# Sending expert results back to their tokens by indirect store, slot by slot, in the second of two fused transformer layers

## The chip, the core and the metric

The kernel is one program on one core of a Trainium2 chip. The metric is the device time of one execution in microseconds (us). Five engines run side by side, each through its own list of instructions in order: PE (TensorE), DVE (VectorE), ACT (ScalarE), POOL (GpSimd) and SP (SyncE, which here only issues DMAs). They wait for each other through semaphores. An engine that waits holds up everything behind it in its own list.

## The reference, cut to what matters

Two layers over 8 sequences of 512 tokens of 128 floats. Each layer is attention over the normalised tokens, then a mixture of 8 experts, each with a residual sum:

```
x = x + attention_0(layernorm(x))     # 16 heads of 8, causal
x = x + experts_0(layernorm(x))       # top 1 of 8 experts, gated SiLU, hidden 512
x = x + attention_1(layernorm(x))     # latent keys and values, rotary, causal
x = x + experts_1(layernorm(x))       # top 2 of 8 experts, ReLU, hidden 512, biases
```

In layer 1 a token's output is the sum over its two experts of probability times `relu(x @ w1[e] + b1[e]) @ w2[e] + b2[e]`. All of it is float32.

## The kernel before, in words

**Batches and halves.** X holds all 4096 tokens on chip, as 32 tiles of 128 tokens by 128 floats, for the whole kernel. Attention goes one sequence (a "batch", 4 tiles) at a time, 16 times in all (8 batches by 2 layers). The experts go by halves: once the attention of four batches (16 tiles) is done, the routing of their 2048 tokens is worked out and their experts run, beside the attention of the following batches. The last half of layer 1 has no attention beside it; it is the end of the kernel.

**One half of the experts.** (1) `route`, `choose` and `places` (PE, ACT, mostly DVE) pick the experts of each token and give each pair of token and choice k a row in a list sorted by expert, padded for each expert to a multiple of 128 rows. The row numbers are `rows_of[g][k]`, one column for each tile. The list has 23 blocks of 128 rows ("slots") in layer 0 and 39 in layer 1, the most that the padding can need. (2) `scatter` (L1090): POOL writes each tile of normalised tokens to its rows of `sorted_in` in DRAM by an indirect DMA of 64 KB, 16 of them in a half of layer 0 and 32 in a half of layer 1 (two for each tile). (3) `fetch` (L1004): SP loads four slots at a time; the first waits for all scatters of the half (L1000). `turn_rows` (L1277) transposes them on PE. (4) For each slot `fetch_w1` (L993) loads the weights of its expert, `first` (L1294) and `second` (L1304) are its two matmul stages on PE, ACT takes the ReLU (L1452), and DVE adds the bias `b2` and writes the result to `rows_out` (L1689, whose records carry L1467). `rows_out` is a ring of three buffers of two slots each. (5) SP stores two slots at a time to `sorted_out` in DRAM (L1014). (6) `combine` (L1100): once all the stores of the half have landed, POOL gathers for each tile and each k the 128 result rows by an indirect DMA into one of four `gathered` buffers, 32 gathers in a half of layer 1, and DVE adds each, times its gate, to X (L1698). A gather waits until the one four before it has been added (L1099). (7) `store` (L1020): SP writes a batch of X to the output, 256 KB.

Before layer 0's first scatter the lists in DRAM are filled with zeros, 39 slots for each half, by ten DMAs from one zero tile (`FILLS`, L964 to L970), as both layers share the lists.

**What sets the order.** Each engine's list is written down before anything runs. `schedule` gives every step a due time from constants (`FIRST_SCORES`, `LENGTHS`, `HURRY`, `SCATTER`, `EXPERTS_AFTER`, `SLOT`, `COMBINE`). `Plan.make_orders` then plays the steps through with costs in us (`PARTS`, `LANDS`) and the dependences of `needs`: again and again it takes the step that can start soonest, and among those that can start equally soon the one with the earliest due time. An indirect DMA counts 1.0 us of POOL there. The costs only choose the order; on the chip the engines follow that order as their semaphores allow.

Due times in layer 1 before the change, worked out from the constants: half 1's 32 scatters at 734 to 766, 1.0 apart; half 0's slots at 685 to 807, 3.12 apart.

Of the kernel before, what the change touches and what calls it, by code (L numbers as in the profile page):

```python
# [58 lines left out]
C_ALL = 332  # L59
# [26 lines left out]
W1_AHEAD = 8.06  # L86
DMA = 16
@dataclass
# [32 lines left out]
class Timetable:  # L121
# [84 lines left out]
    def scatter(self, layer, g, x, at, each):  # L206
        for t in range(QT * x, QT * x + QT):
            for k in range(TOPK[layer]):
                self.put(at, "scatter", layer, g, x, (t, k))
                at += each  # L210
        return at

    def combine(self, layer, g, x, at, each):
        for t in range(QT * x, QT * x + QT):
            for k in range(TOPK[layer]):
                self.put(at, "combine", layer, g, x, (t, k))
                at += each
        if layer == 1:
            self.put(at, "store", layer, g, x)
        return at  # L220
# [16 lines left out]
def schedule():  # L237
# [6 lines left out]
    for n, at in enumerate(FILLS):  # L244
        table.put(at, "fill", x=n)
    starts, end = [], 0.0
    for n, length in enumerate(LENGTHS):
# [20 lines left out]
        if b % GB == GB - 1:  # L268
            g = b // GB
            for x in range(GB):  # L270
                chosen = table.scatter(layer, g, x, chosen, SCATTER[layer][g])
# [23 lines left out]
    "second": (("pe", 0.9), ("dve", 0.24), ("sp", 0.5)), "combine": (("pool", 1.0), ("dve", 0.35)), "store": (("sp", 0.5),)}  # L295

PARTS_L1 = {"first": (("pe", 0.9), ("act", 1.2)), "choose": (("dve", 6.8),), "places": (("pe", 0.2), ("dve", 6.4))}
# [4 lines left out]
         "fetch_w1": 4.6, "fetch": 3.0, "second": 2.4, "combine": 2.5}  # L302
# [12 lines left out]
class Plan:  # L315
# [18 lines left out]
    def parts(self, s):  # L334
# [9 lines left out]
        if s.kind == "second" and s.x % OUT_GROUP != OUT_GROUP - 1 and s.x != SLOTS[s.layer] - 1:  # L344
            return parts[:2]
# [30 lines left out]
    def needs(self, s, engine):  # L376
# [113 lines left out]
        if s.kind == "scatter":  # L490
            return done("dve", of("places", layer, b)) + done("act", of("norm", layer, GB * b + x, "half")) + done("sp", of("fill", x=len(FILLS) - 1)) + (
                done("sp", of("fetch", 0, b, (SLOTS[0] - 1) // 4)) if layer else [])
# [24 lines left out]
        if s.kind == "second":  # L517
            if engine == "pe":
                return done("act" if layer else "dve", of("first", layer, b, x))
            if engine == "dve":  # L520
                out = []
                if x % OUT_GROUP == 0 and s.turn:
                    old = [k for k in self.by_kind["second"] if k.x % OUT_GROUP == 0 and (k.slot, k.turn) == (s.slot, s.turn - 1)][0]
                    out = done("sp", of("second", old.layer, old.b, min(old.x + OUT_GROUP - 1, SLOTS[old.layer] - 1)))
                return out
            return done("dve", self.last_combine(0, b)) if layer and x < OUT_GROUP else []
# [5 lines left out]
        if s.kind == "store":  # L532
            return done("dve", of("combine", 1, b, x, (QT * x + QT - 1, TOPK[1] - 1)))
# [18 lines left out]
    def make_orders(self):  # L552
# [32 lines left out]
        while left:  # L585
# [17 lines left out]
            s.done[engine] = at + us + (LANDS.get(s.kind, 0.0) if engine == "sp" or (engine == "pool" and s.kind in ("scatter", "combine")) else 0.0)  # L603
# [67 lines left out]
def two_layers(nc, d):  # L671
    with ExitStack() as ctx:
# [41 lines left out]
        rows_in = [sb(f"rows_in{i}", [P, SEQ])[:, :] for i in range(2)]  # L714
# [5 lines left out]
        xn_half = sb("xn_half", [P, GT, DIM])  # L720
# [23 lines left out]
        slot_f = sb("slot_f", [1, MAXSLOTS])  # L744
        gates = [[sb(f"gate{g}{k}", [P, GT]) for k in range(2)] for g in range(HALVES)]
        rows_of = [[sb(f"rows_of{g}{k}", [P, GT], I32) for k in range(2)] for g in range(HALVES)]
# [1010 lines left out]
```

## Time and profile before

| | |
|---|---|
| median of 3 runs | 1118.13 us (1117.6 to 1125.34) |
| the profiled execution | 1108.93 us, its span 1107.1 us |
| PE busy | 934.3 us (84%) |
| DVE busy | 691.2 us (62%) |
| ACT busy | 617.4 us (56%) |
| POOL busy | 466.9 us (42%) |
| share of the chain that ended last: PE, DVE, POOL, DMA | 56%, 13%, 10%, 6% |

The span runs from the first instruction to the last event of the execution. A busy share is an average over it; the chain is the work followed back from the last instruction, at each step to what released it. An indirect DMA has two times: POOL's own, while it makes the descriptors, and the time to landing, counted from the issue until the data is there.

### The profile page before, as it was taken

The page shows a single profiled execution, that of the slowest core. Times are in us where ns is not written, and L with a number is a line of the kernel's source. Part 1 is how long each engine was busy: PE and PEld are TensorE (multiplying, and loading weights), DVE is VectorE, ACT ScalarE, POOL GpSimd, SP SyncE. Part 2 cuts the span into 40 slices and gives each one's busy share as a digit, 9 for nine tenths or more (in the row PEclk, how much of TensorE's full clock was granted, in tenths as well). Part 3 has the DMA queues.
Part 4 walks back from the last instruction along what each step waited for, and adds up shares of the span by engine and source line. Part 5 has one row for each costly group of instructions (what it writes and reads, how often), then busy time and mean ns, then how long its engine had stood idle before and what let it go on. Part 6 is the DMA issues. An engine that isn't in the chain of part 4 may idle for free.

```text
span 1107.1 us, 26573 instructions
## 1 busy us (share of the span) xinstructions
PE 934.3 (84%) x9732; PEld 623.3 (56%) x9732; DVE 691.2 (62%) x1454; ACT 617.4 (56%) x1148; POOL 466.9 (42%) x632
## 2 busy tenths in 40 slices
PE   4879989987999998987999888988989997579920
PEld 2434445444887644544877544453447687578920
DVE  4866887787545897987546888888775124023122
ACT  4147786762544576863444576784667864245610
POOL 3033334245111585456111586346862213773046
PEclk9759999996999998998999989997899998889975
DMA  4626433236665124445643214425332456678822
GB/s 134 143 80 185 129 78 80 57 96 187 188 175 153 41 63 117 93 152 166 204 152 106 57 56 117 117 62 144 103 83 70 120 153 171 195 199 235 242 61 74
DMA packets 148045, 139.42 MB, mean 126 GB/s; under 512 B 35056, under 2 KB 126544, under 8 KB 147920
## 3 DMA queue, kind: packets, MB, share of 16 engines
q1 hardware_dynamic: 141776, 125.13, 41.5%
q0 software_dynamic: 6144, 12.60, 4.0%
q8 instruction: 82, 1.34, 0.5%
q14 instruction: 43, 0.35, 0.1%
HBM read 94.82 MB, written 42.86 MB: 124 GB/s over the span
## 4 chain that ended last, share of the span: by engine, by line
PE 56%; DVE 13%; POOL 10%; issue 8%; DMA 6%; ACT 6%; SPq 1%; POOLq 0%; ACTq 0%; DVEq 0%
PE psum L1294 13%; PE psum L1227 11%; PE psum L1304 10%; DVE neg_max L1470 8%; PE psum L1209 5%; PE psum L1185 4%; ACT scratch L1416 4%; POOL sorted_in L1090 4%; DMA gathered<-sorted_out,rows_of 3%; POOL gathered L1100 3%; PE psum L1237 2%; POOL scratch L1077 2%; PE psum L1120 1%; PE psum L1262 1%; PE psum L1188 1%
## 5 line engine op out<-in xcount | busy, mean ns | idle before, releaser
L1470 DVE TENSOR_REDUCE neg_max<-psum 128x2 f32<-128x768 f32 (+3 forms) x352 | 382.5, 1120 | 77.7 <-PE psum L1190 76.1
L1416 ACT ACTIVATE scratch<-psum 128x1024 f32<-128x1024 f32 x320 | 318.3, 1026 | 100.0 <-PE psum L1209 99.3
L1077 POOL TENSOR_SCALAR_AFFINE_SELECT scratch<-scratch 128x512 f32<-128x512 f32 x256 | 159.6, 640 | 357.1 <-ACT scratch L1416 356.7
L1185 PE MATMUL psum<-k_stack,q_stack 48*128 48x128 bf16 (+3 forms) x1024 | 156.3, 328 | 34.7 <-DVE neg_max L1470 23.6
L1227 PE MATMUL psum<-scratch,values 128*32 128x512 f32 (+3 forms) x2048 | 173.7, 464 | 12.1 <-POOL scratch L1077 9.9
L1294 PE MATMUL psum<-rows_t,w_now 128*128 128x128 f32 x1360 | 179.2, 283 | 1.6 <-issue 1.0
L1294 PEld LDWEIGHTS psum<-rows_t,w_now 128*128 128x128 f32 x1360 | 165.1, 196 | 12.0 <-issue 10.3
L1209 PE MATMUL psum<-q_stack,k_stack 51*128 51x512 bf16 (+3 forms) x1024 | 126.6, 315 | 24.8 <-ACT scratch L1416 9.5
L1304 PE MATMUL psum<-w,hidden_t 128*128 x992 | 138.1, 283 | 10.7 <-DVE rows_out L1467 9.2
L1304 PEld LDWEIGHTS psum<-w,hidden_t 128*128 128x128 f32 x992 | 121.8, 193 | 23.0 <-issue 22.5
L1452 ACT ACTIVATE hidden_t<-psum,w_now 128x128 f32<-128x128 f32 x312 | 88.6, 369 | 69.2 <-PE psum L1294 62.5
L1100 POOL DMA_INDIRECT gathered<-sorted_out,rows_of x96 | 92.4, 963 | 82.1 <-DMA sorted_out<-rows_out 51.5
L1090 POOL DMA_INDIRECT sorted_in<-xn_half,rows_of x96 | 93.0, 969 | 51.9 <-issue 26.3
L1188 PE MATMUL psum<-masks_bf 64*128 64x128 bf16 x1024 | 114.5, 235 | 0.0
L1185 PEld LDWEIGHTS psum<-k_stack,q_stack 48*128 48x128 bf16 x1024 | 53.4, 98 | 99.8 <-DVE neg_max L1470 39.0
L1227 PEld LDWEIGHTS psum<-scratch,values 128*32 128x32 f32 x2048 | 57.7, 114 | 80.5 <-issue 47.7
L1190 PE MATMUL psum<-masks_bf 64*128 64x64 bf16 x1024 | 101.4, 200 | 0.0
L1698 DVE SCALAR_TENSOR_TENSOR X<-gathered,gate,X 128x128 f32<-128x128 f32 x96 | 36.2, 377 | 78.4 <-DMA gathered<-sorted_out,rows_of 77.7
L1467 DVE TENSOR_TENSOR rows_out<-psum,w_now 128x128 f32<-128x128 f32 x78 | 22.6, 291 | 97.7 <-PE psum L1304 97.7
L1209 PEld LDWEIGHTS psum<-q_stack,k_stack 51*128 51x128 bf16 x1024 | 36.3, 96 | 80.7 <-issue 35.2
L1312 ACT ACTIVATE ctx_raw<-psum 128x512 f32<-128x512 f32 x64 | 38.1, 595 | 75.1 <-PE psum L1227 75.0
L1190 PEld LDWEIGHTS psum<-masks_bf 64*128 64x128 bf16 x1024 | 56.7, 105 | 32.2 <-issue 9.8
(118 smaller groups left out, 1051.2 us busy)
## 6 DMA issues: line engine op xcount, KB each, us to landing
w_now<-in_w SPq DMA_DIRECT2D x78, 322.0 KB, 3.6
w_now<-in_w SPq DMA_DIRECT2D x46, 512.0 KB, 4.3
q_stack<-q_parts SPq DMA_DIRECT2D x64, 192.0 KB, 4.1
sorted_out<-rows_out SPq DMA_DIRECT2D x60, 128.0 KB, 3.0
rows_in<-sorted_in SPq DMA_DIRECT2D x28, 256.0 KB, 3.3
q_parts<-q_parts SPq DMA_DIRECT2D x16, 384.0 KB, 2.9
k_stack<-k_parts SPq DMA_DIRECT2D x32, 192.0 KB, 3.7
q_parts<-q_parts SPq DMA_DIRECT2D x16, 256.0 KB, 3.1
```

What stands on the lines that cost most here:

```text
L1077: pool.affine_select(out=diag, in_=diag, compare_op=ALU.is_ge, fill=0.0, base=0, pattern=[[0, 4], [1, P]], channel_multiplier=-1).then_inc ...
L1090: pool.indirect_dma_start(sorted_in[g][:, :], bass.IndirectOffsetOnAxis(ap=rows_of[g][k][:, t:t + 1], axis=0), xn_half[:, t, :], None).the ...
L1100: pool.indirect_dma_start(gathered[s.slot][:, :], None, sorted_out[g][0:SLOTS[s.layer] * P, :], bass.IndirectOffsetOnAxis(ap=rows_of[g][k] ...
L1185: pe.matmul(out[:, j * width:end], q_stack[i][rows, pair, t * P:(t + 1) * P], k_stack[i][rows, k_of(layer, pair), 0:width], start=True, st ...
L1188: pe.matmul(out[:, end - P:end], ident_up[half, :], mask_up[half, :], start=False, stop=False)
L1190: ins = pe.matmul(out[:, end - P // 2:end], ident_low[half, :], mask_low[half, :], start=False, stop=True)
L1209: ins = pe.matmul(bank[u.bank + k][:, off:off + SEQ - j * P], k_stack[i][rows, k_of(layer, pair), j * P:(j + 1) * P], q_stack[i][rows, pai ...
L1227: ins = pe.matmul(bank[u.bank][CW * c:CW * c + CW, j * P:SEQ], values[batch_of(s) % 3][:, j, col:col + CW], p[:, c % 2, off:off + SEQ - j ...
L1294: ins = pe.matmul(bank[v.bank][:, c * P:(c + 1) * P], w1_now[layer][w.slot][:, n * FFN + c * P:n * FFN + (c + 1) * P], rows)
L1304: ins = pe.matmul(bank[u.bank][:, 0:P], hidden_t[h.slot][:, k * P:(k + 1) * P], w2[layer][:, bass.ds(e, 1), k * DIM:(k + 1) * DIM].rearran ...
L1416: act.activation(expd[s.slot], psum[:, u.bank:u.bank + 2, :], ACT.Exp, scale=SCALE).then_inc(read[u.bank], 1)
L1470: return dve.tensor_reduce(out=out, in_=in_, axis=AX, op=op, negate=negate)
```

## The change

Layer 1's results no longer go through `sorted_out` and gathers. Rows of `sorted_in` in layer 1 get a 129th float (`ROW`), the place that the result must go to: `C_TOKEN` holds the number of each token in its half, DVE copies it into the new column of `xn_half` in `places`, and after the scatters of k = 0 of a batch a new DVE step, `mark`, adds 2048 to it for k = 1 (after waiting until those scatters have landed). The order of scatters becomes: all 16 of k = 0, then all 16 of k = 1. After each `fetch` DVE waits for the load and copies the 129th column to `goes_to` as integers. For each slot of layer 1 POOL then issues one indirect store of 64 KB from `rows_out` to `returned` in DRAM, at the places of `goes_to`; rows of padding go to a part of `returned` that nothing reads. The 40 stores of layer 1 on SP are gone. `take_back` replaces the 64 gathers of layer 1: for each batch SP issues two plain loads of 256 KB (k = 0 and 1) into the `scratch` that attention uses, after all sends of the half have landed and the last attention is over (`values_made`); DVE waits for both and makes 8 multiply-adds. The lists in DRAM are separate for each layer now: layer 0's have 23 slots (six fills of zeros), layer 1's are filled from a new input `empty_rows` by ten DMAs from DRAM to DRAM, due at 300 to 390. Layer 0 keeps its stores and gathers. Several constants of the due times are other ones.

```diff
-FILLS = (75.0, 80.0, 85.0, 90.0, 95.0, 100.0, 105.0, 115.0, 125.0, 135.0)
+FILLS = ((75.0, 80.0, 85.0, 90.0, 95.0, 100.0), (300.0, 310.0, 320.0, 330.0, 340.0, 350.0, 360.0, 370.0, 380.0, 390.0))
-FIRST_SCORES = 77.59
-AHEAD = (74.87, 87.27)
+FIRST_SCORES = 80.02
+AHEAD = (92.93, 87.27)
-LENGTHS = (41.61, 37.6, 36.08, 35.9, 45.3, 45.3, 45.3, 41.6, 44.0, 44.0, 44.0, 44.0, 34.43, 38.0, 38.0, 38.0)
+LENGTHS = (41.61, 37.6, 37.45, 35.9, 45.3, 45.3, 45.3, 41.35, 44.0, 44.0, 44.0, 44.0, 34.43, 38.0, 38.0, 37.51)
-HURRY = ((30.0, 30.0), (5.73, 36.79))
-SCATTER = ((1.8, 1.1), (1.73, 1.0))
-EXPERTS_AFTER = ((6.0, 5.52), (12.95, 6.0))
-SLOT = ((2.56, 2.6), (3.12, 1.47))
-COMBINE = ((2.44, 2.0), (2.0, 0.2))
+HURRY = ((30.0, 30.0), (2.52, 12.84))
+SCATTER = ((1.8, 1.1), (1.73, 2.32))
+EXPERTS_AFTER = ((6.0, 5.52), (12.95, 21.95))
+SLOT = ((2.47, 2.6), (2.87, 1.47))
+COMBINE = ((3.03, 2.0), (1.31, 0.67))
-W1_AHEAD = 8.06
+W1_AHEAD = 6.52
+ROW = DIM + 1
+RETURNED = 2 * GT * P
...
+    def scatter(self, layer, g, at, each):
+        for k in range(TOPK[layer]):
+            for x in range(GB):
+                if k:
+                    self.put(at - each, "mark", layer, g, x)
+                for t in range(QT * x, QT * x + QT):
+                    self.put(at, "scatter", layer, g, x, (t, k))
+                    at += each
+        return at
...
+        if layer == 1:
+            self.put(at, "take_back", layer, g, x)
+            at += QT * TOPK[layer] * each
+            self.put(at, "store", layer, g, x)
+            return at
...
+    "mark": (("dve", 0.2),), "take_back": (("sp", 1.0), ("dve", 3.3))}
+PARTS_L1 = {"fetch": (("sp", 0.5), ("dve", 0.2)), "second": (("pe", 0.9), ("dve", 0.24), ("pool", 1.0)), ...
...
+        if s.kind == "take_back" and engine == "sp":
+            return done("pool", of("second", 1, b, SLOTS[1] - 1)) + done("pe", of("values", 1, BATCHES - 1, 3, 1))
... SP:
+                    else:
+                        sp.dma_start(out, d["empty_rows"][first * P:(first + n) * P, :]).then_inc(filled[1], DMA)
...
+                elif s.kind == "take_back":
+                    g, x = s.b, s.x
+                    if x == 0:
+                        for slot, value in enumerate(sends_made(g)):
+                            sp.wait_ge(sent_back[slot], value)
+                        sp.wait_ge(values_made, 4 * 2 * BATCHES)
+                    for k in range(2):
+                        first = (k * GT + QT * x) * P
+                        sp.dma_start(taken_back(g, x, k), returned[g][first:first + QT * P, :].rearrange("(t p) d -> p t d", p=P)
+                                     ).then_inc(back_loaded[g][x], DMA)
... POOL:
+                        pool.wait_ge(filled[s.layer], FILLED[s.layer])
+                    if t == QT * x and k == 1:
+                        pool.wait_ge(marked, of("mark", 1, g, x).n + 1)
...
+                elif s.kind == "second":
+                    g, u = s.b, s.uses[0]
+                    x = s.x % OUT_GROUP
+                    slot = of("second", 1, g, s.x - x).slot
+                    pool.wait_ge(places_known, places_read(of("turn_rows", 1, g, s.x // 4)))
+                    pool.wait_ge(read[u.bank], u.after)
+                    pool.indirect_dma_start(returned[g][:, :], bass.IndirectOffsetOnAxis(ap=goes_to[g][:, s.x:s.x + 1], axis=0),
+                                            rows_out[slot][:, x * P:(x + 1) * P], None).then_inc(sent_back[slot], DMA)
... DVE:
+                elif s.kind == "fetch":
+                    n = rows_of_group(1, s.x)
+                    dve.wait_ge(fetched[s.slot], DMA * (s.turn + 1))
+                    dve.tensor_copy(goes_to[b][:, 4 * s.x:4 * s.x + n],
+                                    rows_in[s.slot][:, 0:n * ROW].rearrange("p (t n) -> p t n", t=n)[:, :, DIM]).then_inc(places_known, 1)
+                elif s.kind == "mark":
+                    x = s.x
+                    dve.wait_ge(scattered[x], marks_sent(b, x))
+                    to = xn_half[:, QT * x:QT * x + QT, DIM]
+                    dve.tensor_scalar(to, to, float(GT * P), None, ALU.add, ALU.bypass).then_inc(marked, 1)
+                elif s.kind == "take_back":
+                    g, x = b, s.x
+                    dve.wait_ge(back_loaded[g][x], 2 * DMA)
+                    for k in range(2):
+                        for t in range(QT):
+                            row = X[:, g * GT + QT * x + t, :]
+                            ins = dve.scalar_tensor_tensor(out=row, in0=taken_back(g, x, k)[:, t, :], scalar=gates[g][k][:, QT * x + t:QT * x + t + 1],
+                                                           in1=row, op0=ALU.mult, op1=ALU.add)
+                        if k == 0:
+                            settle(ins)
+                    ins.then_inc(added, 1)
```

## Rows read from the trace of the kernel before

**Rows 1.** The page's forty slices of 27.7 us: busy tenths of PE.

```profile
PE   4879989987999998987999888988989997579920
```

**Rows 2.** Windows by stage: start and end, length, busy us (instructions) by engine, clock, DMA share, GB/s.

```profile
902.00:928.00 26.00, 21.05 (x176) 19.66 (x175) 14.03 (x55) 14.86 (x49) 1.47 (x3) 0.99 0.57 161
...
957.00:972.00 15.00, 0.00 (x0) 0.00 (x0) 0.59 (x2) 0.00 (x0) 11.38 (x12) 0.65 0.49 151
...
1010.00:1060.00 50.00, 49.14 (x419) 47.65 (x419) 8.50 (x30) 30.39 (x103) 0.94 (x1) 1.00 0.77 211
1060.00:1107.00 47.00, 0.00 (x0) 0.00 (x0) 11.43 (x33) 0.00 (x0) 30.35 (x32) 0.54 0.26 69
```

**Rows 3.** The same windows for the second matmul stage alone, line 1304 (8 instructions a slot).

```profile
902.00:928.50 26.50, 9.93 (x72) 8.74 (x72) 0.98 0.56 158
928.50:957.00 28.50, 15.63 (x104) 14.13 (x104) 0.90 0.77 216
...
979.00:1009.90 30.90, 13.96 (x104) 12.51 (x104) 1.00 0.82 229
```

**Rows 4.** Timeline of POOL: start, duration, operation [idle before]; half 1's scatters, first gathers.

```profile
927.74 1.04 POOL L1090 DMA_INDIRECT sorted_in<-xn_half,rows_of  x1 [21.39 <-DVE rows_of L1654]
...
966.98 0.96 POOL L1090 DMA_INDIRECT sorted_in<-xn_half,rows_of  x1 [0.30 <-issue]
968.24 0.99 POOL L1100 DMA_INDIRECT gathered<-sorted_out,rows_of  x1 [0.31 <-issue]
```

**Rows 5.** Timeline of PE around the start of half 1's experts.

```profile
972.23 2.27 PE L1277 MATMUL psum<-consts,rows_in 128*128 128x128 f32 x8 [15.32 <-DMA rows_in<-sorted_in]
...
979.07 1.06 PE L1304 MATMUL psum<-w,hidden_t 128*128 x8
```

**Rows 6.** The chain that ended last: start us, us, what; experts of half 1.

```profile
1005.22 3.90 DMA gathered<-sorted_out,rows_of
...
1009.41 0.29 DVE rows_out L1467
...
1009.95 1.15 PE psum L1304 x8
```

**Rows 7.** The same chain, from the last slot to the end.

```profile
1058.71 1.17 PE psum L1304 x8
...
1059.90 0.30 DVE rows_out L1467
...
1060.22 1.54 DMA sorted_out<-rows_out
...
1062.35 0.94 POOL gathered L1100
...
1103.77 0.35 DVE X L1698
```

**Rows 8.** DMA issues: number, KB each, median us to landing.

```profile
rows_in<-sorted_in SPq DMA_DIRECT2D x28, 256.0 KB, 3.3
...
sorted_in<-xn_half,rows_of POOLq DMA_INDIRECT x96, 2.2
```

**Rows 9.** Line 1077 (causal masks) alone, beside half 0's experts.

```profile
840.00:902.00 62.00, 11.72 (x19) 1.00 0.43 120
```

**Rows 10.** Timeline of POOL: half 0's scatters, the first and the sixteenth.

```profile
755.74 1.08 POOL L1090 DMA_INDIRECT sorted_in<-xn_half,rows_of  x1 [1.26 <-DVE rows_of L1654]
...
787.31 0.96 POOL L1090 DMA_INDIRECT sorted_in<-xn_half,rows_of  x1 [0.30 <-issue]
```

**Rows 11.** The costliest groups of the page: DVE's row maxima, and its adds of gathered rows.

```profile
L1470 DVE TENSOR_REDUCE neg_max<-psum 128x2 f32<-128x768 f32 (+3 forms) x352 | 382.5, 1120 | 77.7 <-PE psum L1190 76.1
...
L1698 DVE SCALAR_TENSOR_TENSOR X<-gathered,gate,X 128x128 f32<-128x128 f32 x96 | 36.2, 377 | 78.4 <-DMA gathered<-sorted_out,rows_of 77.7
```

More of the change, by code:

```diff
@@ L204, in after @@
         return at + 23.0 + 4.0 * layer
[L206 to L210, printed above, removed]
+    def scatter(self, layer, g, at, each):
[6 more added lines that the diff above has]
+                    at += each
         return at
     def combine(self, layer, g, x, at, each):
-        for t in range(QT * x, QT * x + QT):
[L215 to L219, printed above, removed]
+        if layer == 1:
[3 more added lines that the diff above has]
+            return at
+        for t in range(QT * x, QT * x + QT):
+            self.put(at, "combine", layer, g, x, (t, 0))
+            at += each
         return at
@@ L243, in schedule @@
         table.put(REST_AT + 0.4 * n, "load_rest", x=n)
-    for n, at in enumerate(FILLS):
-        table.put(at, "fill", x=n)
+    for layer, times in enumerate(FILLS):
+        for n, at in enumerate(times):
+            table.put(at, "fill", layer, x=n)
     starts, end = [], 0.0
@@ L269, in schedule @@
             g = b // GB
-            for x in range(GB):
-                chosen = table.scatter(layer, g, x, chosen, SCATTER[layer][g])
+            chosen = table.scatter(layer, g, chosen, SCATTER[layer][g])
             end = table.experts(layer, g, max(chosen + EXPERTS_AFTER[layer][g], end + 12.0), SLOT[layer][g])
@@ L490, in needs @@
         if s.kind == "scatter":
-            return done("dve", of("places", layer, b)) + done("act", of("norm", layer, GB * b + x, "half")) + done("sp", of("fill", x=len(FILLS) - 1)) + (
-                done("sp", of("fetch", 0, b, (SLOTS[0] - 1) // 4)) if layer else [])
+            return done("dve", of("places", layer, b)) + done("act", of("norm", layer, GB * b + x, "half")) + done("sp", of("fill", layer, x=len(FILLS[layer]) - 1)) + (
+                done("dve", of("mark", 1, b, x)) if y[1] else [])
+        if s.kind == "mark":
+            return done("pool", of("scatter", 1, b, x, (QT * x + QT - 1, 0)))
         if s.kind == "fetch_w1":
@@ L792, in two_layers @@
         W2_LOADED = EXPERTS * DMA
-        ZERO_FILLED = len(FILLS) * DMA
+        FILLED = [len(times) * DMA for times in FILLS]
         def batch_of(s):
@@ L1024, in _ @@
                 sp.wait_ge(out_stored, DMA * BATCHES)
-            for slot, value in enumerate(stores_made(1, 1)):
+            for slot, value in enumerate(stores_made(HALVES - 1)):
                 sp.wait_ge(stored[slot], value)
@@ L1683, in _ @@
                     dve.wait_ge(full[u.bank], u.filled)
[L1684 to L1685 removed]
+                    if x == 0 and stores_before(head, 0):
+                        dve.wait_ge(stored[head.slot], stores_before(head, 0))
+                    if x == 0 and stores_before(head, 1):
+                        dve.wait_ge(sent_back[head.slot], stores_before(head, 1))
                     if layer == 0:
```

135 lines of the change are left out of this document (80 added, 55 removed).

## The prediction

> **What bounds the kernel now.** I read the page's slices first: PE is 8 or 9 tenths busy nearly everywhere until the last six slices, where it falls to 5 and 7 and then to 2 and 0 [rows 1]. So up to about 900 us PE has work waiting, and an edit elsewhere is worth little there. The windows by stage divide the end. From 957 to 972 us PE does nothing (0.00 of 15.00), from 1010 to 1060 it is full (49.14 of 50.00), from 1060 to the end it is idle again for 47 us while POOL works 30.35 of them [rows 2]. Three things lie behind these windows. First, the scatters of half 1: POOL issues 32 from 927.74 to the last at 966.98 [rows 4], which is (966.98 - 927.74) / 31 = 1.266 us each, and PE's first transposes start at 972.23, after an idle time of 15.32 [rows 5]. Second, the gathers of half 0, behind those scatters on POOL [rows 4]: in the chain, DVE's write of a slot's result at 1009.41 stands behind a gather's landing of 3.90 us, and PE's next stage begins at 1009.95 [rows 6]. Third, the 32 gathers of half 1: the last slot's result is written at 1059.90, the first gather starts at 1062.35, the last add at 1103.77 [rows 7].
>
> **The sum** is made in the profiled execution, 1108.93 us with a span of 1107.1. The median of the three runs, 1118.13, is 9.2 above it; I take the difference over to that median.
>
> *The tail.* Now from the end of the last write, 1059.90 + 0.30, to 1107.1: 46.9 us [rows 7]. After the change: POOL's wake 0.3 and a store whose nearest row is the scatter, also 64 KB and indirect, 2.2 us to landing [rows 8], makes 2.5. SP's wake 0.2. Then eight loads of 256 KB in the form of the row fetches, 3.3 us alone [rows 8]. Beside each other they are bound by bandwidth: the experts' windows move 211 GB/s [rows 2], 262 KB at that rate is 1.25 us. So the pair of batch 0 is there after 3.3 + 1.25 = 4.6 and the last pair after 3.3 + 7 x 1.25 = 12.1. DVE has 8 adds a batch; one takes 0.377 on the mean and 0.35 here [rows 7, 11], 2.8 a batch, 11.2 for four. DVE ends at 4.6 + 11.2 = 15.8 (by the loads it would be 12.1 + 2.8 = 14.9). The last output takes 1107.1 - 1104.1 = 3.0 [rows 7]. Sum 2.5 + 0.2 + 15.8 + 3.0 = 21.5; gain **25.4**. From below: adds that overlap at 0.27, then bandwidth binds, 20.6. From above: loads at half the rate, 2.5 each, end at 20.8, then 2.8 and 3.0: 29.3.
>
> *Half 1's experts.* With half 0's gathers gone the slots run at their own pace. From 1009.95 to 1058.71 it is 25 slots in 48.76 us, 1.95 each [rows 6, 7]. From 979 to 1009.9 it was 104 / 8 = 13 slots in 30.9 us [rows 3], 25.4 at that pace: gain **5.5**. The start-up (972.23 to 979.07 [rows 5], at a lower clock: 0.65 is granted in the idle window before it [rows 2]) stays. POOL's send is 1.27 a slot, under 1.95, and falls beside PE's work. Half 0's take_back needs its last send, 32 adds (11.2 us of DVE) and 2 MB of loads; they find PE idle in front of half 1's start, so I cost them at nothing. If half 0's sends end so late that this cover is gone, they lie in half 1's run, where DVE is busy 8.50 of 50 [rows 2], and cost at most their 11.2.
>
> *The scatters of half 1, the part that speaks against the change.* POOL was free for them. Now it also sends half 0's slots, and the fetch waits for the last scatter. Line 1304 has 9 slots from 902 to 928.5 and 13 from 928.5 to 957 [rows 3]; the last of the nine gets its result out only behind `places`, so 14 sends fall in the time of the scatters. The order on POOL is by due time when both are ready: sends 26 to 38 are due at 772 to 807 (692 + 2.87 for each slot, and 5.5), scatters at 761 to 833 (2.32 apart). So all sends are written ahead of the last 12 scatters, and the scatters end 14 x 1.266 = **17.7** later. From below: scatters first, 0. From above: POOL waits at each send for PE's slot, 14 x 1.95 = 27.3. I take 17.7, since per slot one send and one and a half scatters are 3.2 us, more than PE's 1.95, so POOL is the late one and doesn't wait. PE's idle time becomes 15 + 17.7 = 33.
>
> *Earlier sends.* 17 of half 0's slots come before 902 and 8 before 928, 25 x 1.27 = 32 us of POOL. Beside attention POOL is a fifth busy (11.72 of 62 with masks [rows 9]). 17 sends make a third more; a mask that finds one in front of it waits 0.6 on the mean, so 19 masks lose about 4 us together, and PE has slots to do meanwhile. I count **1**; if each is paid in full with its landing order, 8; nothing in the trace makes it a gain beyond the SP time of 20 stores, which no one waits for.
>
> *Fills, columns, copies.* Ten fills of zeros become six, and ten of 528 KB are added in a stretch that PE fills; 0 to 3, I take 0. A longer row changes no count of DMAs. The copy of 39 x 128 places, the token column (0.1 to 0.2 on the way to the scatters) and the marks are 0.5 together if nothing waits; what waits is a rival. The Trainium skill has a rule against the longer rows: in "DMA: Bandwidth & Descriptors", "How a descriptor splits into AXI transactions", a descriptor that doesn't start on a 256-byte boundary starts its first read at the boundary below. A row of 516 bytes then costs about 24 beats where 512 took 16, an estimate from that section; by it the first fetch of half 1 would take 1.5 times as long, and the sum would be 1.7 us worse. No row shows an unaligned load, so the sum does without it.
>
> Sum: -25.4 - 5.5 + 17.7 + 1 + 0.5 = **-11.7**, which is 1106.4 on the median, 1106 rounded.
>
> **Rivals.**
> (B) *The scatters give more back.* POOL's order is worked out with 1.0 us for a send and 0.9 + 0.9 for a slot, the chip needs 1.27 and 1.95, and a DVE waiting in `mark` for a landing holds the results that the sends wait for. At the upper bound of the term, 27.3, and 3 for the early sends: -25.4 - 5.5 + 27.3 + 3 + 0.5 = -0.1; half way it is -6. Time 1112 to 1118, no change that counts. For: the due times put sends and scatters side by side. Against: POOL is the later of the two there.
> (C) *Slower: DVE waits for DMAs in half 0's scatters.* `mark` waits on DVE for POOL's scatters of k = 0, 16 of which take from 755.74 to 788 [rows 10], 32 us with other work between, where the written order allows 1.0 us each. Behind a waiting mark stand the row maxima, 1.12 us each [rows 11], and attention's PE behind them. Each us that DVE stands in this stretch counts in full, since the experts of half 0 haven't begun. It decides when the waits sum to more than 11.7 + 11.2 = 23 us. At 25 the time is 1131. Against: a mark is due 12 scatters before its own k = 1 scatter, so the planner may write it late.
> (D) *The term doesn't exist.* If the order puts scatters first, PE works through its 15 us of idle time and the sends trail: 0 in place of 17.7, -29.4, 1089.
>
> **How the numbers follow.** A measurement of this kernel can tell about 1%, 11.2 us, from no change. Forecast (A), 1106 with its own range from 1097 to 1111: 0.42. B: 0.36. C: 0.16. D: 0.06. A lies right at the edge of 1%, so part of its chance belongs to "within 1%" and nearly none of B's to faster: faster 0.42 + 0.06 less 0.04 = 0.44; within 1%: 0.36 + 0.04 + 0.02 (a mild C) = 0.42; slower 0.14. The range must hold A, B and the mild part of C: 1094 (the lower bounds of the tail and of the sends) to 1126; outside are D and the rest of C, 0.2.
>
> **What would show it.** The last `rows_out` is written 11 to 13 us later than 1060; from there to the end it is 21 us, not 47. Between the first and last scatter of half 1 POOL has 14 sends and 57 us instead of 40. PE's idle time ahead of half 1's experts is about 33 us. The pace from the first slot on is 1.95. The start of half 0's experts and the end of attention (902) stay within 3 us; if attention ends much later and DVE shows waits for `sorted_in`, it is C. If the scatters end at 968 as now, it is D. I am wrong above all if POOL waits in the middle of the scatters for PE, or if the loads of take_back are far slower beside each other than 1.25 us.

## The result, and the profile after

The changed kernel takes **1102.59 us** in the median of 18 runs (1096.22 to 1109.76); the kernel before, in 18 runs beside it, 1113.32 us (1101.77 to 1125.34). The ratio is 0.9919, 95% interval 0.989 to 0.9948: faster, by 0.5 to 1.1%. By the ratio that is 9.0 us less, where 11.7 were forecast, and 1106 was forecast from a first median of 1118.13, which the 18 runs put at 1113.32. The 11.7 taken from 1113.32 would have been 1101.6, so part of the nearness of 1106 to 1102.59 is that first median. The time lies in the range. The gain of 0.8% lies within the 1% that the prediction counted as no change, which it gave 0.42; it gave "faster" 0.44.

The profiled execution has a span of 1101.7 us against 1107.1. The windows by stage, cut at the changed kernel's own landmarks (columns as in [rows 2]: start and end, length, busy us and instructions of PE, PE's weight loads (PEld), DVE, ACT and POOL, then clock, DMA share, GB/s; "clock" is the granted TensorE clock as a share of full speed):

```profile
913.00:939.00 26.00, 21.41 (x180) 20.02 (x178) 14.11 (x57) 15.07 (x49) 9.95 (x11) 1.00 0.56 161
939.00:968.00 29.00, 25.96 (x195) 25.02 (x196) 5.26 (x21) 13.29 (x46) 22.01 (x23) 0.88 0.68 184
968.00:1002.00 34.00, 0.62 (x6) 0.43 (x4) 9.43 (x34) 0.00 (x0) 22.48 (x23) 0.53 0.56 166
1002.00:1083.00 81.00, 80.10 (x663) 77.69 (x663) 13.05 (x49) 49.45 (x166) 36.04 (x38) 0.96 0.71 199
1083.00:1101.70 18.70, 0.00 (x0) 0.00 (x0) 9.14 (x33) 0.00 (x0) 1.30 (x2) 0.59 0.60 176
```

Against [rows 2]: the first window does the same PE work as before, 21.41 us for 21.05, but begins at 913 instead of 902. PE's idle window is 34 us long instead of 15. Then half 1's experts fill PE for 80.10 of 81 us, and what follows the last slot is 18.7 us instead of 47.

The timeline of POOL shows why the idle window has grown (columns as in [rows 4], which these answer):

```profile
939.09 0.96 POOL L1147 DMA_INDIRECT sorted_in<-xn_half,rows_of  x1 [2.99 <-DVE rows_of L1753]
...
944.13 0.96 POOL L1156 DMA_INDIRECT returned<-rows_out,goes_to  x1 [0.30 <-issue]
945.40 0.95 POOL L1147 DMA_INDIRECT sorted_in<-xn_half,rows_of  x1 [0.30 <-issue]
946.66 0.96 POOL L1156 DMA_INDIRECT returned<-rows_out,goes_to  x1 [0.30 <-DVE goes_to L1556]
...
996.36 0.96 POOL L1147 DMA_INDIRECT sorted_in<-xn_half,rows_of  x1 [0.30 <-issue]
```

Scatters (L1147) and sends (L1156) are mixed until 981 us, and the last 12 scatters stand alone, as the due times said. There is the same 0.30 us between any two, so POOL never waits. From the first scatter to the last it is 57.3 us, where it was 39.2 [rows 4]: that is 14 sends of 1.266 us, 17.7, and 0.3 more. On PE's side (rows like [rows 5]):

```profile
967.47 1.15 PE L1371 MATMUL psum<-w,hidden_t 128*128 x8 [0.42 <-ACT hidden_t L1519]
1002.12 2.00 PE L1344 MATMUL psum<-consts,rows_in 128*128 128x128 f32 x8 [33.50 <-DMA rows_in<-sorted_in]
1003.92 4.77 PE L1361 MATMUL psum<-rows_t,w_now 128*128 128x128 f32 x24
1008.53 1.06 PE L1371 MATMUL psum<-w,hidden_t 128*128 x8
```

The idle time is 33.50, the forecast said "about 33". The chain that ended last, from the last slot to the end (columns as in [rows 6]; it answers to [rows 7]):

```profile
1080.41 0.91 PE psum L1371 x8
...
1083.96 2.23 DMA returned<-rows_out,goes_to
...
1086.21 0.38 SPq L1073
...
1087.74 4.41 DMA scratch<-returned
...
1092.17 1.15 DVE X L1572 x4
...
1093.35 2.20 DVE X L1572 x8
...
1095.57 2.20 DVE X L1572 x8
```

No POOL instruction stands between two adds any more. DVE goes through the four batches almost without a pause; the timeline of DVE there (same columns as POOL's) has one wait before the first batch and 0.18 before the rest:

```profile
1089.68 2.31 DVE L1572 SCALAR_TENSOR_TENSOR X<-scratch,gate,X 128x128 f32<-128x128 f32 x8 [6.47 <-DMA scratch<-returned]
...
1092.17 6.76 DVE L1572 SCALAR_TENSOR_TENSOR X<-scratch,gate,X 128x128 f32<-128x128 f32 x24 [0.18 <-DMA scratch<-returned]
```

The balance of the two profiled executions, in stages that add up to the span:

| stage | before | after | difference | forecast |
|---|---|---|---|---|
| start to half 1's first scatter | 927.74 | 939.09 | +11.4 | +1.5 |
| first scatter to PE's first transposes of half 1 | 44.5 | 63.0 | +18.5 | +17.7 |
| to the end of the last `rows_out` | 88.0 | 81.1 | -6.9 | -5.5 |
| to the end of the span | 46.9 | 18.5 | -28.4 | -25.4 |
| sum | 1107.1 | 1101.7 | -5.4 | -11.7 |

Three of the four stages are as forecast within about 3 us. The first is not: attention's last projection ends 11 us later, and nothing in the forecast put it there (it begins at 913.0, before at 901.6). The experiments go after that, and after the largest loss, the 18.5.

### The profile page after: what moved, and what is told of

Read it like the earlier page. It is cut to its first block, busy times and chain, and to the rows that moved or that the text cites. A ratio compares the mean times of both kernels' runs of the same rounds, so it can differ in the third digit from the quotient of the medians.

```text
span 1101.7 us, 26611 instructions
## 1 busy us (share of the span) xinstructions
PE 942.7 (86%) x9732; PEld 626.8 (57%) x9732; DVE 695.3 (63%) x1484; ACT 617.3 (56%) x1148; POOL 480.5 (44%) x646
## 4 chain that ended last, share of the span: by engine, by line
PE 60%; DVE 11%; POOL 11%; ACT 7%; issue 7%; DMA 3%; SPq 1%; POOLq 0%; DVEq 0%; ACTq 0%
PE psum L1361 14%; PE psum L1293 12%; PE psum L1371 11%; DVE neg_max L1537 7%; POOL sorted_in L1147 6%; PE psum L1275 5%; PE psum L1251 4%; ACT scratch L1483 4%; PE psum L1222 2%; POOL scratch L1136 2%; PE psum L1303 2%; PE psum L1186 1%; PE psum L1254 1%; PE psum L1328 1%; PE psum L1344 1%
## 5 line engine op out<-in xcount | busy, mean ns | idle before, releaser
L1293 PE MATMUL psum<-scratch,values 128*32 128x512 f32 (+3 forms) x2048 | 183.2, 486 | 13.6 <-POOL scratch L1136 10.9
L1251 PE MATMUL psum<-k_stack,q_stack 48*128 48x128 bf16 (+3 forms) x1024 | 153.8, 324 | 35.7 <-DVE neg_max L1537 24.0
L1156 POOL DMA_INDIRECT returned<-rows_out,goes_to x78 | 75.1, 962 | 88.6 <-DVE rows_out L1534 66.4
L1293 PEld LDWEIGHTS psum<-scratch,values 128*32 128x32 f32 x2048 | 60.3, 117 | 86.7 <-issue 53.8
L1147 POOL DMA_INDIRECT sorted_in<-xn_half,rows_of x96 | 93.2, 971 | 32.3 <-issue 25.8
L1534 DVE TENSOR_TENSOR rows_out<-psum,w_now 128x128 f32<-128x128 f32 x78 | 22.9, 294 | 115.0 <-PE psum L1371 111.8
L1100 POOL TENSOR_TENSOR ln_small<-ln_small,consts 128x4 f32<-128x4 f32 x40 | 42.2, 1054 | 31.5 <-DVE ln_small L1604 31.2
```

Of the source, the lines that this page charges most:

```text
L1147: pool.indirect_dma_start(sorted_in[s.layer][g][:, :], bass.IndirectOffsetOnAxis(ap=rows_of[g][k][:, t:t + 1], axis=0), xn_half[:, t, 0:wi ...
L1251: pe.matmul(out[:, j * width:end], q_stack[i][rows, pair, t * P:(t + 1) * P], k_stack[i][rows, k_of(layer, pair), 0:width], start=True, st ...
L1293: ins = pe.matmul(bank[u.bank][CW * c:CW * c + CW, j * P:SEQ], values[batch_of(s) % 3][:, j, col:col + CW], p[:, c % 2, off:off + SEQ - j ...
```

## The experiments

The experiments ran in three groups. The kernels of a group shared one chip and their runs of the kernel before, and each has its own ratio to it. In the first group the kernel before took 1202.0 us, in the others 1112.64 and 1115.3. The first and the second group both carry the chip number 6, the third 9, so it isn't shown that the slow group ran on another chip than the second. Kernels of different groups are compared by their ratios, and the first group with care. Where a text below speaks of "that chip" or "the slower chip", read the first group.

### First group: where the constants, the fills and the order stand

**scatters_first**, sends written behind all scatters of half 1; only due times differ:

```diff
-SCATTER = ((1.8, 1.1), (1.73, 2.32))
-EXPERTS_AFTER = ((6.0, 5.52), (12.95, 21.95))
+SCATTER = ((1.8, 1.1), (1.73, 0.1))
+EXPERTS_AFTER = ((6.0, 5.52), (12.95, 92.99))
```

> The changed kernel with one thing altered: the 32 scatters of half 1 are due 0.1 apart instead of 2.32, so POOL has all of them ahead of half 0's remaining sends (the due time of half 1's experts is kept). Theory: sends and scatters share POOL, and each of the 14 sends written ahead of the last scatter puts off half 1's experts by 1.266 us. Then the scatters take 40.5 us again instead of 57.3, and PE's first transposes of half 1 come some 44.5 us after the first scatter instead of 63.0. The ring of six result slots makes PE leave about 8 slots of half 0 (15.6 us) for afterwards, which lie in what was idle time: the end comes 3 to 17 us earlier, 1 to 13 us if the sends left over then crowd half 1's first slots. Rival: PE's idle time is only moved behind half 0's late slots, since half 1's first slot can't pass them in PE's order: no difference, within 4 us of the changed kernel.

**old_times**, the changed kernel with all due-time constants of the kernel before:

```diff
-FIRST_SCORES = 80.02
-AHEAD = (92.93, 87.27)
+FIRST_SCORES = 77.59
+AHEAD = (74.87, 87.27)
...
-HURRY = ((30.0, 30.0), (2.52, 12.84))
-SCATTER = ((1.8, 1.1), (1.73, 2.32))
+HURRY = ((30.0, 30.0), (5.73, 36.79))
+SCATTER = ((1.8, 1.1), (1.73, 1.0))
...
```

> The changed kernel with every due-time constant of the kernel before (FIRST_SCORES, AHEAD, LENGTHS, HURRY, SCATTER, EXPERTS_AFTER, SLOT, COMBINE, W1_AHEAD). It also has the scatters of half 1 ahead of half 0's last sends. Theory 1: the 11 us by which attention of layer 1 ends later in the changed kernel's trace come from the new constants; then attention's last projection is back at 902 +- 3 us and the time is that of scatters_first less up to 11 us. Theory 2: they come from the change itself (fills from DRAM, DVE's waits for fetches, sends on POOL); then the last projection stays at 910 to 914. Theory 3: they are the scatter of single executions; then the projections of all these kernels vary by some us with no order.

**before_new_times**, the kernel before with the new constants for all that is ahead of layer 1's experts:

```diff
-FIRST_SCORES = 77.59
-AHEAD = (74.87, 87.27)
+FIRST_SCORES = 80.02
+AHEAD = (92.93, 87.27)
...
-SLOT = ((2.56, 2.6), (3.12, 1.47))
-COMBINE = ((2.44, 2.0), (2.0, 0.2))
-W1_AHEAD = 8.06
+SLOT = ((2.47, 2.6), (3.12, 1.47))
+COMBINE = ((3.03, 2.0), (2.0, 0.2))
+W1_AHEAD = 6.52
```

> The kernel before, with the changed kernel's constants for everything ahead of half 0 of layer 1's experts (FIRST_SCORES, AHEAD, LENGTHS, W1_AHEAD, layer 0's SLOT and COMBINE); stores, gathers, fills are as before. Theory 1 (new constants cost 11 us by the end of attention): last projection at 910 to 914, time 5 to 11 us over the kernel before. Theories 2 and 3: last projection at 898 to 905, time within 4 us of the kernel before.

**fills_early**, layer 1's fills moved on SP's queue:

```diff
-FILLS = ((75.0, ...), (300.0, 310.0, 320.0, 330.0, 340.0, 350.0, 360.0, 370.0, 380.0, 390.0))
+FILLS = ((75.0, ...), (120.0, 125.0, 130.0, 135.0, 140.0, 145.0, 150.0, 155.0, 160.0, 165.0))
```

> The changed kernel with layer 1's ten fills from DRAM due at 120 to 165 instead of 300 to 390; only SP's order differs. If the fills' traffic holds up the attention of batches 5 and 6 of layer 0 (where the changed kernel lost 8 us of its lead), the projections of those batches come up to 8 us earlier and the time is 3 to 8 us less. If the fills cost nothing, as the prediction took them, it is within 3 us of the changed kernel.

Measured, as ratios to the kernel before on that chip, with 95% intervals: scatters_first 0.9679 (0.9624 to 0.9735), old_times 0.9585 (0.9526 to 0.9644), fills_early 0.9685 (0.9628 to 0.9743), before_new_times **1.0081** (1.0045 to 1.0117). The last is the clearest: the new constants alone, with none of the change, cost the kernel before 0.8%, 1211.55 us for 1202.0. It is what theory 1 says. old_times points the same way, 10 us under scatters_first (1154.21 and 1164.3), from which it differs by constants alone. The single executions don't decide it: their last projections are at 962 (before_new_times), 949 (scatters_first) and 953 (old_times), 35 to 60 us later than those of the same or nearly the same kernels outside this group (901.6, 913.9 and 900.6). fills_early (1163.94) is level with scatters_first; the changed kernel itself is not in this group, so it says nothing on either against it. The second group has it.

### Second group: the same questions beside the changed kernel

**changed_again**, no edit:

> The changed kernel once more, as the yardstick of this comparison, since the four kernels before ran on a chip on which the kernel before takes 1202 us instead of 1113. If that chip's long waits for DMAs hit the kernel before harder (it has 40 stores and 64 gathers more), the ratio there would be near 0.968, that of fills_early; on a chip like the first it is 0.992 again. In the trace: PE's idle time ahead of half 1 at 33 us, the end 18 to 19 us behind the last rows_out; attention's last projection at 902 to 913 tells how much of the 11 us was one execution's.

**scatters_first_2**, the edit of scatters_first:

> The changed kernel with half 1's scatters ahead of half 0's last sends, now beside the changed kernel itself. Theory (each send ahead of the last scatter costs 1.266 us): the scatters take 40.5 us, and the end is 3 to 13 us earlier. Rival (PE's half 0 slots, held by the ring of six results, come later by as much): within 4 us. On the slower chip PE stood 16 us for rows_out there, which speaks for the rival.

**attention_old**, the changed kernel with the old constants ahead of layer 1's experts, the new ones for those:

```diff
-FIRST_SCORES = 80.02
-AHEAD = (92.93, 87.27)
+FIRST_SCORES = 77.59
+AHEAD = (74.87, 87.27)
...
-SLOT = ((2.47, 2.6), (2.87, 1.47))
-COMBINE = ((3.03, 2.0), (1.31, 0.67))
-W1_AHEAD = 6.52
+SLOT = ((2.56, 2.6), (2.87, 1.47))
+COMBINE = ((2.44, 2.0), (1.31, 0.67))
+W1_AHEAD = 8.06
```

> The changed kernel with the old constants for everything ahead of half 0's experts of layer 1 (FIRST_SCORES, AHEAD, LENGTHS, W1_AHEAD, layer 0's SLOT and COMBINE); the constants of layer 1's experts stay new, so sends and scatters of half 1 stay interleaved. Theory 1 (the new attention constants cost about 10 us, as the kernel before lost 0.8% with them): 6 to 12 us faster than the changed kernel, last projection 8 us or more earlier. Theory 2 (the change itself delays attention): the same time within 3 us.

**old_times_2**, the edit of old_times:

> The changed kernel with all old constants, beside the changed kernel itself. If the attention constants cost 10 us and the order of scatters nothing, it equals attention_old within 3 us. If the order of scatters is worth something of its own, it is faster than attention_old by that, 3 to 13 us.

| kernel | median us | ratio to before | 95% interval |
|---|---|---|---|
| changed_again | 1102.65 | 0.9909 | 0.9875 to 0.9943 |
| scatters_first_2 | 1103.37 | 0.9919 | 0.989 to 0.9949 |
| attention_old | 1093.7 | 0.9832 | 0.9784 to 0.9879 |
| old_times_2 | 1093.55 | 0.9845 | 0.9793 to 0.9897 |

The changed kernel repeats its first result. The old attention constants win 9.0 us in the median, as theory 1 expected (6 to 12); the slowest of the six runs of attention_old (1097.81) is faster than the fastest of the nine of changed_again (1099.26). The last projection came 6.5 us earlier (909.5 after 916.0), a little short of the 8 that were named; in single executions it is a rough gauge, since changed_again's own is 3 us from the changed kernel's first.

The order of scatters is worth **nothing** that these intervals can show (they are 0.3 to 0.5% wide to each side): scatters_first_2 is level with changed_again, old_times_2 (scatters first too) with attention_old (not). The theory is wrong and its rival right. The timeline of PE in scatters_first_2 (a profiled execution of 1110.06 us, its slowest of 12) shows where the time goes:

```profile
954.47 1.06 PE L1371 MATMUL psum<-w,hidden_t 128*128 x8
955.36 2.84 PE L1361 MATMUL psum<-rows_t,w_now 128*128 128x128 f32 x24
983.23 3.78 PE L1371 MATMUL psum<-w,hidden_t 128*128 x16 [25.02 <-DVE rows_out L1534]
988.73 1.72 PE L1344 MATMUL psum<-consts,rows_in 128*128 128x128 f32 x7 [1.72 <-DVE rows_out L1534]
```

and POOL's there:

```profile
939.91 0.96 POOL L1147 DMA_INDIRECT sorted_in<-xn_half,rows_of  x1 [2.96 <-DVE rows_of L1753]
...
979.06 0.95 POOL L1147 DMA_INDIRECT sorted_in<-xn_half,rows_of  x1 [0.31 <-issue]
980.32 0.96 POOL L1156 DMA_INDIRECT returned<-rows_out,goes_to  x1 [0.30 <-issue]
```

The scatters do end after 39.2 us, as before. But a result slot comes free only when its send has landed, and the ring holds six. So PE stands from 958 to 983 with half 0 unfinished, waiting on DVE, and DVE waits 21.32 us for a send to land before it writes the next results at 982.68. PE's idle time has not gone, it has moved ahead of half 0's last slots.

### Third group: breaking the tie, splitting the constants, sizing the tail

**big_ring**, old_times with a ring of 16 result slots in layer 1, placed in the second-stage weights of layer 0 (what the edit adds to that of old_times, shortened):

```diff
+OUT_RING = (3, 8)
...
-                          "second": ("out", 3), ...
+                          "second": (f"out{s.layer}", OUT_RING[s.layer]), ...
...
-        rows_out = [sb(f"rows_out{i}", [P, OUT_GROUP * P])[:, :] for i in range(3)]
+        rows_out = [[sb(f"rows_out{i}", [P, OUT_GROUP * P])[:, :] for i in range(3)],
+                    [w2[0][:, :, :].rearrange("p e n -> p (e n)")[:, i * OUT_GROUP * P:(i + 1) * OUT_GROUP * P] for i in range(OUT_RING[1])]]
```

> old_times with one thing more: layer 1's ring of result slots has 16 slots instead of 6 (it lies in layer 0's second-stage weights, which layer 1 doesn't read). Half 1's scatters are ahead of half 0's last sends. Theory: scatters and sends are tied by the ring; with scatters first PE runs out of result slots after 6 and stands 25 us for rows_out. With 16 it can finish half 0 during the scatters, half 1 starts some 45 us after the first scatter, and the 14 late sends fit beside half 1's slots, which leave POOL 1.93 - 1.27 = 0.66 us each: 8 to 17 us faster than old_times (0.984 of the kernel before becomes 0.97 to 0.977). Rival: the late sends hold back half 0's take_back and half 1's first sends on POOL and DVE so that half 1 runs slower by as much: within 3 us of old_times.

Measured: **1083.21 us**, ratio 0.9718 (0.9676 to 0.976), where old_times_2 has 0.9845 (0.9793 to 0.9897). The theory holds: 1.3% of the kernel before more, 14 us by the ratios and 10 by the medians (the two ran in different groups; their intervals do not overlap). It is the fastest kernel of the study, 2.8% under the kernel before. Timeline of PE in it:

```profile
955.61 1.15 PE L1373 MATMUL psum<-w,hidden_t 128*128 x8 [0.43 <-ACT hidden_t L1521]
972.99 2.06 PE L1346 MATMUL psum<-consts,rows_in 128*128 128x128 f32 x8 [16.23 <-DMA rows_in<-sorted_in]
...
996.25 1.16 PE L1363 MATMUL psum<-rows_t,w_now 128*128 128x128 f32 x8 [2.99 <-DMA w_now<-in_w]
...
1000.86 1.58 PE L1363 MATMUL psum<-rows_t,w_now 128*128 128x128 f32 x8 [2.56 <-DMA w_now<-in_w]
```

PE is through with half 0 at 957, during the scatters, and half 1 starts 44.7 us after the first scatter (928.32), as in the kernel before; the idle time is 16.23. From there to the last result (1062.13) it is 89.1 us, not the 81.1 of the changed kernel. So of the 18 us won in front, 8 are given back inside: the late sends and half 0's take_back now fall in half 1's first slots, and PE waits for weights there, 2.99 and 2.56 us in the lines shown. On SP's queue four loads of take_back are issued from 988.53 on, ahead of the next load of weights at 992.69. The deep ring with the changed kernel's own order of scatters was not run.

**starts_old** and **slots_old**, the two halves of attention_old's edit on the changed kernel:

```diff
 starts_old:
-FIRST_SCORES = 80.02
-AHEAD = (92.93, 87.27)
-LENGTHS = (41.61, 37.6, 37.45, ..., 41.35, ..., 37.51)
+FIRST_SCORES = 77.59
+AHEAD = (74.87, 87.27)
+LENGTHS = (41.61, 37.6, 36.08, ..., 41.6, ..., 38.0)
 slots_old:
-SLOT = ((2.47, 2.6), (2.87, 1.47))
-COMBINE = ((3.03, 2.0), (1.31, 0.67))
-W1_AHEAD = 6.52
+SLOT = ((2.56, 2.6), (2.87, 1.47))
+COMBINE = ((2.44, 2.0), (1.31, 0.67))
+W1_AHEAD = 8.06
```

> The changed kernel with FIRST_SCORES, AHEAD and LENGTHS of the kernel before (when attention and its preparations are due); layer 0's SLOT and COMBINE and W1_AHEAD stay new. If these three carry the 9 us that attention_old won: about 1094 where the changed kernel has 1103. If the others do: 1103.

> The counterpart of starts_old: layer 0's SLOT and COMBINE and W1_AHEAD of the kernel before, FIRST_SCORES, AHEAD and LENGTHS new. If these carry the 9 us: about 1094; if not, 1103. If each alone gives part or neither does, it is the order that they make together.

Measured: starts_old 1095.31 us, ratio 0.9806 (0.9759 to 0.9853); slots_old 1102.95, ratio 0.9918 (0.9882 to 0.9955). The loss lies in FIRST_SCORES, AHEAD and LENGTHS, which were not tried one by one; the other three constants make no difference that can be seen.

The traces show where the 9 us lie, if one takes the time between two projections (L1319; L1253 in the kernel before, L1321 in big_ring) instead of the last one. From batch 1's to batch 3's in layer 1, ten traces, all but those of the first group, give (times in us; half_the_adds follows below):

| FIRST_SCORES, AHEAD, LENGTHS | from batch 1's to batch 3's | PE instructions | PE busy | PE idle | clock |
|---|---|---|---|---|---|
| old (before, attention_old, old_times_2, starts_old, big_ring) | 101.4 to 106.0, mean 102.8 | 987 or 988 | 89.8 to 94.8, mean 91.0 | 11.2 to 12.5 | 0.90 to 0.95 |
| new (after, changed_again, scatters_first_2, slots_old, half_the_adds) | 106.5 to 115.0, mean 111.1 | 985 or 986 | 92.9 to 103.3, mean 98.7 | 11.8 to 13.6 | 0.82 to 0.92 |

The stretch is 8.3 us longer with the new constants, and PE is busy 7.7 us longer in it with the same work; its idle time is nearly the same. So this loss is not a wait: PE is slower at the same work, at a lower granted clock. From 600 to 760 us PE is busy as long in the changed kernel (first line) as in attention_old (second), with 113 instructions fewer:

```profile
600.00:760.00 160.00, 142.61 (x1482) 80.52 (x1480) 125.09 (x268) 99.85 (x162) 78.28 (x108) 0.89 0.27 71
600.00:760.00 160.00, 142.60 (x1595) 81.99 (x1597) 131.51 (x289) 105.29 (x172) 81.76 (x114) 0.95 0.30 78
```

In the changed kernel the clock is 0.52 from 681.7 to 697.7 us, behind 8 us in which PE worked 5.41; at the same distance from batch 1's projection PE worked 6.71 of 8 in attention_old, and the next 16 us had 0.95. Three traces of the first group with the new constants have 113.8 us for the stretch at a clock of 0.87, and old_times 110.3 at 0.88, a smaller difference. No run holds the clock and changes the order, so that the order of steps brings the clock down is the reading that these traces suggest, not one that a run has shown by itself.

**half_the_adds**, the changed kernel without the adds of k = 1 of half 1, and without DVE's wait for its own adds of k = 0 there (`settle`):

```diff
-                    for k in range(2):
+                    for k in range(2 - g):
...
-                        if k == 0:
+                        if k == 0 and g == 0:
```

> The changed kernel without the adds of k = 1 of half 1's take_back: DVE makes 16 of the last 32 adds, the loads are the same. If DVE's adds bind the tail, as the prediction reckoned, the end comes 16 x 0.28 = 4.6 us earlier, less what the loads then bind: 3 to 5 us (ratio to the kernel before 0.987). If the loads bind, it comes 1.2 us earlier at most (the last batch's four adds).

Measured: 1098.03 us, ratio 0.9848 (0.9805 to 0.9891) for changed_again's 0.9909 (0.9875 to 0.9943) in the second group: 4.6 us by the medians, 6.8 by the ratios, whose intervals overlap. The timeline of DVE is more exact:

```profile
1084.82 0.29 DVE L1534 TENSOR_TENSOR rows_out<-psum,w_now 128x128 f32<-128x128 f32 x1 [1.29 <-PE psum L1371]
...
1091.69 1.14 DVE L1572 SCALAR_TENSOR_TENSOR X<-scratch,gate,X 128x128 f32<-128x128 f32 x4 [6.58 <-DMA scratch<-returned]
...
1094.58 1.14 DVE L1572 SCALAR_TENSOR_TENSOR X<-scratch,gate,X 128x128 f32<-128x128 f32 x4 [1.75 <-DMA scratch<-returned]
...
1097.63 1.14 DVE L1572 SCALAR_TENSOR_TENSOR X<-scratch,gate,X 128x128 f32<-128x128 f32 x4 [0.41 <-DMA scratch<-returned]
```

Now each batch waits for its loads, and the last pair is there 9.5 us after the first issue (1088.13). From the last result, ready at 1085.11, to the last add, done at 1098.77, it is 13.7 us, where the changed kernel needs 15.7 (1083.21 to 1098.94). So neither expectation is met as it stands (3 to 5 us, or 1.2 at most): the adds bind the tail when there are 32, but the loads stand only 2 us behind them. The wins of the medians are larger than these 2 us. The edit touches nothing ahead of the tail, so I take the rest for the scatter of the runs and of the groups; no run shows that.

## Why the prediction was right or wrong, point by point

**The tail** was right in mechanism and 3 us too small (25.4 forecast, 28.4 measured). Its pieces: send 3.0 us from the last result to its landing (2.5 forecast, and 0.2 for SP), the first pair of loads 3.5 (4.6), adds 9.3 (11.2), output 2.8 (3.0). The most mis-sized piece is the adds: 24 in a row take 6.76 us, 0.28 each. One record lasts 0.35 in such a row too (0.347 is the median of all 64 adds, 0.35 in [rows 7]), so neighbours overlap, and their sum is not the time of a row. I had named 0.27 for the lower bound, but its 20.6 still holds 2.8 us for the last eight adds; with 0.27 throughout it is about 20. The loads were over-sized as well: I had the last pair 12.1 us after the first issue, and half_the_adds has it after 9.5.

**Half 1's pace** was right: 38 slots from 1008.53 to 1081.73, 1.93 each, forecast 1.95. The gain of 6.9 for 5.5 is this and a start-up of 6.4 us for 6.8. Half 0's take_back, costed at nothing, cost nothing: DVE's 32 adds lie at 988 to 997, in PE's idle window.

**The scatters of half 1** were right as the changed kernel stands: 14 sends, 17.7 us forecast, 18.0 measured between first and last scatter. Reading the due times told the order that POOL followed. Rival (B), that POOL would wait for PE's slots or DVE's marks and give 27.3 us back, did not come: POOL had no such wait. That the two profiled executions differ by 5.4 us, near (B)'s half-way value of 6, is chance; the loss lies elsewhere, as "What the prediction left out" says. What was wrong is the step beside it, *"from below: scatters first, 0"*, and with it rival (D). It took the order on POOL to be the cause. scatters_first_2 and old_times_2 show that the order is worth nothing as long as the ring has six slots; big_ring shows that the deep ring with scatters first is worth 1.3%. I had reckoned (D) with PE working through its idle time, without asking where its results would go.

**Earlier sends, fills, marks, copies** were forecast at 1.5 us together, and by old_times_2 and big_ring they cost about nothing: with all constants old and the change made, their last projections begin at 900.6 and 902.2, and that of the kernel before at 901.6. Single projections scatter, but from batch 3's to the last, where half 0's marks and most of its early sends lie, it is 173.3 to 176.2 us in the four traces with the change and the old attention constants, and 174.2 in the kernel before. Rival (C) did not come: DVE waited for scatters ahead of a mark three times in the whole execution, 7.9 us in all, and the two longest (2.49 and 3.88) lie at 966 and 975, where attention is over. The longer rows landed in 3.4 us for 258 KB, after 3.3 for 256 KB [rows 8]; among half 1's fetches alone the medians are 3.8 and 3.7. The trace does not show the 1.5 times that I had worked out from the Trainium skill ("DMA: Bandwidth & Descriptors", "How a descriptor splits into AXI transactions"). That estimate took the worst start for every row: by that section's rule a row of 516 bytes takes 17 to 24 beats by where it starts, 20.5 on the mean, 1.3 times 16, an estimate as well.

```profile
rows_in<-sorted_in SPq DMA_DIRECT2D x18, 258.0 KB, 3.4
...
scratch<-returned SPq DMA_DIRECT2D x16, 256.0 KB, 4.6
```

**What the prediction left out** is the price of the new constants of the plan. It used them to read the order of sends and scatters and gave them no price anywhere else, in effect zero. That step failed: it forecast the end of attention at 902 within 3 us, and it came at 913 and 916, and by the largest amount of all: +9.0 us in the medians (attention_old against changed_again); the first row of the balance shows it as +11.4 in one execution. before_new_times shows the same loss without the change, starts_old that it lies in FIRST_SCORES, AHEAD and LENGTHS, and the table of the third group that 8.3 us of it lie, at a lower clock, between batches 1 and 3 of layer 1. The change by itself is worth 0.9845 (0.9793 to 0.9897, old_times_2), 17 us, and was forecast at 11.7: the forecast of the time was nearly met by luck, because two errors, a gain some 5 us too small and a loss of 9 us left out, go against each other.

**Open:** which of the three constants, and which change in the order of steps, goes with the lower clock between batches 1 and 3 of layer 1. Single projections place nothing, since with the old attention constants they already lie up to 10 us apart (batch 0 of layer 1: 545.1 in big_ring, 555.5 in starts_old); the length of the stretch does, but the clock in it differs between executions of one kernel too (0.85 in after, 0.92 in changed_again). That the price of the fills is nothing rests on the first group, where fills_early and scatters_first are level, and on scatters_first_2 being level with the changed kernel; it wasn't tried directly.

## What to carry to other kernels

When an instruction is moved into an engine's queue ahead of one that others wait for, count the instructions, not the shares: 14 times 1.266 us, 17.7, came out as 18.0. But before reordering two groups on one queue, follow the results of the group that is put last to the buffers they hold; here the order was worth nothing with the shallow ring, and 1.3% came with the deep one. And a change that comes with re-tuned constants is two changes: run the old constants with the new code, and the new constants with the old code, before giving the code the credit or the blame. When the same instructions keep PE busy longer and its idle time is the same, look at the granted clock before looking for a wait.

## What the runs showed of the hardware that was not expected

In ten traces, 985 to 988 PE instructions of the same work took 89.8 to 103.3 us of PE's busy time, at granted clocks from 0.95 down to 0.82 (the table of the third group). The projection of layer 1, eight matmuls, took 2.08 us at a clock of 0.50 (692.72 us in the changed kernel's trace) and 1.06 at 1.00 (912.96).

In the first group the kernel before took 1202.0 us (1192.55 to 1213.66 in 17 runs) instead of 1113. The engines' instructions lasted as long there (gathers 956 ns on the mean, 963 in the first profiled execution, scatters 968 and 969), but ACT and DVE had waits of up to 26.2 and 24.3 us in before_new_times whose releaser the profile can't name. The chain of before_new_times puts 9.4% of its 1206.3 us down to such releasers:

```profile
by line: PE psum L1294 12.5%; PE psum L1227 10.7%; PE psum L1304 9.5%; another core or an unknown queue 9.4%; DVE neg_max L1470 8.8%; issue 6.3%; PE psum L1209 5.0%; PE psum L1185 4.4%; ACT scratch L1416 3.7%; PE psum L1156 2.7%; POOL gathe
```

What held the engines up there stays open, and so does whether it was the chip: the second group, on the same chip number, had 1112.64 us for the same kernel. The change is worth more in the first group: old_times has 0.9585 there and 0.9845 in the second, so a ratio of two kernels, too, belongs to the conditions in which it was taken.
